# A recommendation tower on one Trainium2 core: its gram products split by weight columns into fourths of the TensorE array

## The chip, the core and the metric

The kernel runs on one NeuronCore of one Trainium2 chip. The metric is the device time of one launch in microseconds (us). TensorE (PE, its weight loads PEld) multiplies, VectorE (DVE) and ScalarE (ACT) work elementwise, GpSimd (POOL) and SyncE (SP) here issue transfers.

## The reference

There are 2048 samples. For each, 39 rows of 32 features are looked up in 39 tables. Everything is float32.

```python
def _cin_layer(h0, h, W):                      # Wr = W.reshape(F0, Fi, K)
    return jnp.einsum('bid,bjd,ijk->bkd', h0, h, Wr)
conv1 = _cin_layer(x, x, W1)                   # x: (2048, 39, 32), W1: (39*39, 128)
hidden1, final1 = conv1[:, :64, :], conv1[:, 64:, :]
conv2 = _cin_layer(x, hidden1, W2)             # W2: (39*64, 128)
z = jnp.sum(jnp.concatenate([final1, conv2], axis=1), axis=2)
h = jnp.concatenate([z, dense_ctx], axis=1)    # 192 + 16
h = jnp.maximum(h @ W_top1 + b_top1, 0.0)      # 512
h = jnp.maximum(h @ W_top2 + b_top2, 0.0)      # 256
y = h @ W_top3
```

Since `z` is summed over the 32 features, `final1` and `conv2` need only two small products per sample, summed over features: hidden with x (64 by 39) and x with x (39 by 39). These are the gram products that the change touches. `hidden1` itself is needed with its features.

## The kernel before

The samples go in 16 tiles of 128, each tile in two chunks of 64 samples, so there are 32 chunks. Two tiles are a pair, and each engine has a `pair_body` with `k` from 0 to 3 for the chunk in the pair and `t` from 0 to 6 for its seven steps. All queues are in order, and the order within them is written out by hand.

What one chunk goes through:

- POOL looks up 33 of the 39 tables for a tile by indirect transfers (L392), into `emb`, two buffers. It starts a tile's look-ups when the tile two earlier has been turned by DVE (`xt_ready`) and stored (`spilled`).
- SP stores the tile to DRAM in another order, 8 transfers of small rows (L341, "spill"), waits until they have landed, and then loads shifted copies of x, 14 transfers of 312 KB for each chunk (L359), into `copies`. Each load waits until DVE has made its last use of that buffer, two chunks earlier (one chunk for the last copy). The next tile's spill stands behind these 28 loads in the same queue.
- DVE multiplies pairs of copies (L750, four instructions a step; L745 in the last two chunks) into a ring of four places, three steps ahead of the step that PE is at. DVE also turns x (L726) and the hidden rows (L772).
- PE's `hidden_step` (L416) multiplies two weights by two blocks side by side, one in each column half of the array, and accumulates in `hidden`.
- ACT sorts the finished hidden rows (L586, L592), DVE turns them into `turned`, and one chunk later PE forms the gram products in `gram_group` (L439), after the steps `t` = 2, 4 and 6, for 3, 3 and 2 of eight parts. That is 6, 6 and 4 "places"; a place is one pair of matmuls, in the upper and the lower 64 rows of the array. ACT's `gram_copy` (L627) takes each group out of PSUM into `arena`; there is one PSUM place for all groups, so that the next group waits for it (`gram_out`).
- ACT's `spread_x` (L615) writes the diagonal operand `xdiag` for the coming gram products, part 0 at `t` = 4 and part 1 at `t` = 6.
- In odd chunks PE's `final_sums` (L456, then L461) follows each of the three gram groups. In even chunks `layer1` (L471, L472) follows the second and `layer2` (L480) the third; `layer3` (L487) stands in the odd chunk after the first group. The relus are ACT's `relu1` (L648) and `relu2` (L654). The first `final_sums` of an odd chunk also waits for `relu2` (`l2_act`), because both use the same PSUM bank.

Each float32 matmul shows in the trace as two PE records and two weight loads. A gram matmul before has 64 rows, 103 weight columns (64 of the summed hidden rows and 39 of x) and 78 streamed columns.

Of the kernel before, what the change touches and what calls it, by code (L numbers as in the profile page):

```python
# [16 lines left out]
HID = 64  # L17
# [16 lines left out]
LAST = STEPS - 1  # L34
# [9 lines left out]
GS = HID + F  # L44
GM = 2 * F
# [49 lines left out]
def since(count, first):  # L95
    return count >= first


def build(nc, dense, ids, hot_ids, hot_rows, tables, W_top1, b_top1, W_top2, b_top2, W_top3, W1, W2,
          fold_c, to_columns_c, to_samples_c, xt, hot_t, y_out):  # L100
    with ExitStack() as ctx:
        def sb(name, shape, dt):
            return ctx.enter_context(nc.sbuf_tensor(name, shape, dt))
# [7 lines left out]
        gst = [turned[:, u] for u in range(2)]  # L111
# [3 lines left out]
        xdiag = sb("xdiag", [P, HALF, GM], F32)  # L115
# [292 lines left out]
        def _(pe):  # L408
# [12 lines left out]
            def gram_group(k, chunk, j):  # L421
                if j == 0:
                    pe.wait_ge(hid_turned, 2 * chunk + 2)
                if j in (0, 2):
                    pe.wait_ge(xdiag_ready, 2 * chunk + 1 + j // 2)
                group = N_GROUPS * chunk + j
                into = gram
                if chunk == CHUNKS - 1 and j < 2:
                    into = hidden[:, j]
                elif chunk == CHUNKS - 1:  # L430
                    pe.wait_ge(gram_out, N_GROUPS * chunk)
                    pe.wait_ge(gram2_out, 1)
                elif since(group, 1):
                    pe.wait_ge(gram_out, group)
                for r in range(2 * GROUPS[j]):
                    place = 2 * sum(GROUPS[:j]) + r
                    for half in range(2):
                        rows = slice(64 * half, 64 * half + 64)
                        mm = nc.tensor.matmul(into[0:GS, half, r * GM:(r + 1) * GM],  # L439
                                              gst[k // 2][rows, 2 * place + k % 2, 0:GS],  # L440
                                              xdiag[rows, place, :], start=True, stop=True)
                mm.then_inc(gram_filled, 1)

            def final_sums(tile, u, j):
# [80 lines left out]
            for t in range(TILES):  # L525
                mm = nc.tensor.matmul(hidden[0:DENSE, t // 8, t // 4 % 2, (t % 4) * P:(t % 4 + 1) * P],
                                      dense_in[:, t, :], to_columns[:, :], start=True, stop=True)
# [34 lines left out]
            for p in range(1, PAIRS):  # L562
                pair_body(p, False)
            gram_group(3, CHUNKS - 1, 0)
            gram_group(3, CHUNKS - 1, 1)
            layer1(TILES - 2)
            gram_group(3, CHUNKS - 1, 2)
# [10 lines left out]
        def _(act):  # L578
            def sort_hidden(k, chunk):
                if since(chunk, 1):  # L580
                    act.wait_ge(hid_turned, 2 * chunk - 1)
                for bank in range(BANKS):
                    act.wait_ge(hid_pairs, pairs_done(chunk, LAST, bank))
                    for c in range(2):
                        q, other = 2 * c + bank, 2 * c + 1 - bank
                        op = nc.scalar.activation(hid_high[32 * q:32 * q + 32, :],  # L586
                                                  hidden[32 * other:32 * other + 32, k % 2, bank, :], ACT.Copy)
                op.then_inc(hid_sorted, 1)
                act.wait_ge(hid_sorted, 2 * chunk + 1)
                for q in (1, 3):  # L590
                    rows = slice(32 * q, 32 * q + 32)
                    op = nc.scalar.activation(hidden[rows, k % 2, 0, :], hidden[rows, k % 2, 1, :], ACT.Copy)  # L592
                op.then_inc(hid_sorted, 1)
# [10 lines left out]
            def spread_x(k, tile, chunk, part):  # L604
                places = slice(0, SPREAD) if part == 0 else slice(SPREAD, HALF)
                if part == 0 and k % 2 == 0:
                    act.wait_ge(xt_ready, tile + 1)
                    if tile + 2 < TILES:
                        act.wait_ge(spilled[tile % 2], 16 * SPILLS * (tile // 2 + 1))
                        place(tile + 2)  # L610
                if since(chunk, 1):
                    act.wait_ge(gram_filled, N_GROUPS * (chunk - 1) + 2 + part)
                for q in range(Q):
                    rows = slice(32 * q, 32 * q + 32)
                    op = nc.scalar.activation(  # L615
                        xdiag[rows, places, q % 2 * F:(q % 2 + 1) * F],
                        gst[k // 2][rows, 2 * places.start + k % 2:2 * places.stop:2, HID:GS], ACT.Copy)
                op.then_inc(xdiag_ready, 1)

            def gram_copy(k, tile, chunk, j):  # L620
                act.wait_ge(gram_filled, N_GROUPS * chunk + j + 1)
                if k % 2 == 0 and j == 0 and since(tile, 2):
                    act.wait_ge(fin_done, tile - 1)
                cols, g = gram_places(k, chunk, j)

                def copy(out, i, rows, last_copy=False):
                    op = nc.scalar.activation(out[:, :, cols].rearrange("p h (u b) -> p h u b", u=2), g[rows, i], ACT.Copy)  # L627
                    if last_copy:
                        op.then_inc(gram_out, 1)

                if not late(chunk, j):
                    copy(gram2[0:HID, :], slice(0, F, 2), slice(0, HID))
                    copy(gram2[HID:P, 0:FH - 1], slice(1, F, 2), slice(0, HID))
                for c in range(4):
                    rows = slice(c * SLOT, (c + 1) * SLOT)
                    copy(gram1[rows, 0:len(range(c, F, 4))], slice(c, F, 4), slice(HID, HID + SLOT))
                    rows = slice(c * SLOT, c * SLOT + TOP)
                    copy(gram1[rows, F1A:F1A + len(range(c, TOP, 4))], slice(SLOT + c, F, 4),
                         slice(HID + SLOT, GS), last_copy=(c == 3))

            def fin_half_copy(tile):
                act.wait_ge(fin_done, tile + 1)
                nc.scalar.activation(fin_half[:, :], fin_final1[64:128, :], ACT.Copy).then_inc(fin_half_out, 1)

            def relu1(tile):
                act.wait_ge(l1_done, tile + 1)
                for m in range(T1 // P):
                    op = nc.scalar.activation(act1[:, m, :], outs1[:, m, :], ACT.Relu, bias=bias1[:, m:m + 1])  # L648
                op.then_inc(l1_act, 1)

            def relu2(tile):
                act.wait_ge(l2_done, tile + 1)
                for m in range(T2 // P):
                    op = nc.scalar.activation(act2[:, m, :], outs2[:, m, :], ACT.Relu, bias=bias2[:, m:m + 1])  # L654
                op.then_inc(l2_act, 1)

            def pair_body(p, first):
                for k in range(4):
                    chunk, tile, done = 4 * p + k, 2 * p + k // 2, 2 * p - 2 + k // 2
                    for t in range(STEPS):  # L660
                        if t == LAST:
                            sort_hidden(k, chunk)
                            if chunk == CHUNKS - 1:
                                fin_half_copy(TILES - 2)
                        if t in (2, 4, 6) and (k or not first):
                            gram_copy((k - 1) % 4, 2 * p + (k - 1) // 2, chunk - 1, t // 2 - 1)
                        if k % 2 == 0 and not first and t == 4:
                            relu1(done)
                        if k == 1 and not first and t == LAST:
                            fin_half_copy(2 * p - 1)  # L670
                        if k == 3 and p < PAIRS - 1 and t == LAST:
                            fin_half_copy(2 * p)
                        if t in (4, 6):
                            spread_x(k, tile, chunk, t // 2 - 2)
                        if k % 2 == 0 and not first and t == LAST:
                            relu2(done)

            act.dma_start(row_number[:, :], hot_rows).then_inc(hot_loaded, 16)
            for n, f in enumerate(HOT):
# [21 lines left out]
            place(1)  # L701
            act.wait_ge(cleared, 3)
            pair_body(0, True)
            act.wait_ge(mlp_loaded, 16 * 7)
            for p in range(1, PAIRS):
                pair_body(p, False)
# [231 lines left out]
```

## Time and profile before

| | |
|---|---|
| time, median of 3 runs | 867.06 us (863.35 to 873.03) |
| the profiled execution's own time | 862.46 us |
| its span, first to last instruction | 860.7 us |
| mean granted TensorE clock | 0.966 |
| PE busy, of the span | 766.1 us (89%) |
| DVE busy | 702.1 us (82%) |
| ACT busy | 569.4 us (66%) |
| POOL busy | 536.1 us (62%) |
| gram products L439 (into `sums`): PE, weight loads | 115.1 us, 101.3 us |

An engine's busy time counts each moment once, however many of its records run in it. PE records are pipelined and start before the one ahead has ended, so that the spacing of their starts says more of a group's pace than the length of a record.

### The profile page before, as it was taken

The page shows a single profiled execution, that of the slowest core. Times are in us where ns is not written, and L with a number is a line of the kernel's source. Part 1 is how long each engine was busy: PE and PEld are TensorE (multiplying, and loading weights), DVE is VectorE, ACT ScalarE, POOL GpSimd, SP SyncE. Part 2 cuts the span into 40 slices and gives each one's busy share as a digit, 9 for nine tenths or more (in the row PEclk, how much of TensorE's full clock was granted, in tenths as well). Part 3 has the DMA queues.
Part 4 walks back from the last instruction along what each step waited for, and adds up shares of the span by engine and source line. Part 5 has one row for each costly group of instructions (what it writes and reads, how often), then busy time and mean ns, then how long its engine had stood idle before and what let it go on. Part 6 is the DMA issues. An engine that isn't in the chain of part 4 may idle for free.

```text
span 860.7 us, 17408 instructions
## 1 busy us (share of the span) xinstructions
PE 766.1 (89%) x6518; PEld 457.8 (53%) x6518; DVE 702.1 (82%) x1105; ACT 569.4 (66%) x1565; POOL 536.1 (62%) x535
## 2 busy tenths in 40 slices
PE   2696776899999998999899999999998989999996
PEld 1695122465556463645455564656464535556566
DVE  4957786899798979888889989898979787889850
ACT  0202244878777876767787878787876758787872
POOL 7777777777776777677676777777777676000000
PEclk9889896999999999999999999999999989999999
DMA  5759888788888888787878887888888788878300
GB/s 116 208 132 246 218 195 249 180 284 197 240 229 227 242 192 247 184 255 167 289 204 258 199 292 201 281 207 241 218 204 231 176 244 189 256 199 267 125 1 1
DMA packets 173739, 178.38 MB, mean 207 GB/s; under 512 B 144299, under 2 KB 154489, under 8 KB 156055
## 3 DMA queue, kind: packets, MB, share of 16 engines
q1 hardware_dynamic: 153243, 164.76, 67.6%
q0 software_dynamic: 16992, 8.73, 6.8%
q10 hardware_dynamic: 3420, 3.79, 1.5%
q8 instruction: 51, 0.84, 0.4%
q14 instruction: 33, 0.27, 0.1%
HBM read 161.97 MB, written 15.24 MB: 206 GB/s over the span
## 4 chain that ended last, share of the span: by engine, by line
PE 23%; ACT 22%; DMA 19%; DVE 17%; SPq 14%; issue 5%; DVEq 0%; ACTq 0%
DMA copies<-xt 14%; DVE blocks L750 13%; PE hidden L416 10%; ACT arena L627 9%; SPq L341 7%; PE sums L456 6%; SPq L359 6%; ACT xdiag L615 5%; PE sums L439 4%; ACT hid_high L586 4%; DMA blocks<-hot_t 3%; ACT hidden L592 2%; ACT act L648 2%; DMA xt<-emb 1%; DVE copies L805 1%
## 5 line engine op out<-in xcount | busy, mean ns | idle before, releaser
L392 POOL DMA_INDIRECT emb<-in_tbl,ids_tile x531 | 535.9, 1009 | 192.9 <-issue 188.8
L750 DVE TENSOR_TENSOR blocks<-copies 117x512 f32<-117x512 f32 x840 | 525.0, 693 | 96.4 <-PE hidden L416 45.1
L416 PE MATMUL hidden<-blocks,w_pairs 117*64 117x512 f32 x1792 | 439.3, 617 | 42.3 <-DVE blocks L750 40.0
L627 ACT ACTIVATE arena<-sums 64x480 f32<-64x480 f32 (+2 forms) x936 | 292.8, 313 | 178.4 <-PE sums L439 154.1
L416 PEld LDWEIGHTS hidden<-blocks,w_pairs 117*64 117x64 f32 x1792 | 145.0, 139 | 258.4 <-DVE blocks L750 112.8
L439 PEld LDWEIGHTS sums<-xdiag,turned 64*103 64x103 f32 x2000 | 101.3, 171 | 86.7 <-issue 39.4
L615 ACT ACTIVATE xdiag<-turned 32x468 f32<-32x468 f32 (+1 forms) x256 | 119.0, 465 | 3.4
L439 PE MATMUL sums<-xdiag,turned 64*103 64x78 f32 x2000 | 115.1, 261 | 6.8 <-ACT arena L627 5.7
L456 PE MATMUL sums<-arena,w_fin 128*128 128x128 f32 x640 | 81.7, 285 | 10.3 <-ACT act L654 9.7
L586 ACT ACTIVATE hid_high<-hidden 32x512 f32<-32x512 f32 x128 | 75.2, 588 | 16.3 <-PE hidden L416 14.3
L456 PEld LDWEIGHTS sums<-arena,w_fin 128*128 128x128 f32 x640 | 76.2, 197 | 13.4 <-issue 11.4
L726 DVE STREAM_TRANSPOSE turned<-emb 128x1248 f32<-128x1248 f32 x16 | 39.4, 2462 | 0.0
L592 ACT ACTIVATE hidden<-hidden 32x512 f32<-32x512 f32 x64 | 36.2, 566 | 1.4
L745 DVE TENSOR_TENSOR blocks<-copies 117x1024 f32<-117x1024 f32 x28 | 32.4, 1218 | 5.2 <-PE hidden L416 5.1
L480 PE MATMUL sums<-act,wt 128*128 128x128 f32 x256 | 32.8, 282 | 1.6 <-ACT act L648 1.2
L480 PEld LDWEIGHTS sums<-act,wt 128*128 128x128 f32 x256 | 29.8, 192 | 3.0 <-ACT act L648 1.4
L461 PE MATMUL sums<-arena,w_fin 128*64 128x128 f32 x384 | 30.9, 279 | 0.0
L471 PE MATMUL sums<-z_conv,wt1a 128*128 128x128 f32 x128 | 26.4, 287 | 1.1 <-DVE z_rest L781 1.1
L805 DVE TENSOR_SCALAR copies<-blocks,row_number 125x2048 bf16<-125x2048 int16 (+1 forms) x32 | 21.5, 742 | 5.1 <-DMA blocks<-hot_t 5.1
L461 PEld LDWEIGHTS sums<-arena,w_fin 128*64 128x64 f32 x384 | 23.4, 136 | 3.1
L472 PE MATMUL sums<-z_rest,wt1b 80*128 80x128 f32 x128 | 24.8, 274 | 0.0
L515 PE MATMUL sums<-turned,copies 125*128 125x96 bf16 x240 | 14.5, 236 | 9.4 <-DVE copies L805 4.7
(72 smaller groups left out, 294.9 us busy)
## 6 DMA issues: line engine op xcount, KB each, us to landing
copies<-xt SPq DMA_DIRECT2D x448, 312.0 KB
xt<-emb SPq DMA_DIRECT2D x64, 152.0 KB
emb<-in_tbl,ids_tile POOLq DMA_INDIRECT x531
xt<-emb SPq DMA_DIRECT2D x32, 104.0 KB
arena<-in_fold ACTq DMA_DIRECT2D x1, 2688.0 KB, 15.0
xt<-emb SPq DMA_DIRECT2D x32, 56.0 KB
blocks<-hot_t SPq DMA_DIRECT2D x3, 500.0 KB
turned<-hot_t SPq DMA_DIRECT2D x2, 468.8 KB
```

The source lines that it names most:

```text
L341: sp.dma_start(xt[u, row:row + end - first, h, :].rearrange("f (s d) -> s f d", d=D), emb[u][h::2, first * D:end * D].rearrange("s (f d) - ...
L392: pool.indirect_dma_start(out=emb[u][:, f * D:(f + 1) * D], out_offset=None, in_=tables[f], in_offset=bass.IndirectOffsetOnAxis(ap=ids_til ...
L416: mm = nc.tensor.matmul(hidden[64 * c:64 * c + 64, k % 2, bank, :], w_pairs[0:ROWS, t, bank * HALF_HID:bank * HALF_HID + HID], blocks[0:RO ...
L439: mm = nc.tensor.matmul(into[0:GS, half, r * GM:(r + 1) * GM], gst[k // 2][rows, 2 * place + k % 2, 0:GS], xdiag[rows, place, :], start=Tr ...
L456: mm = nc.tensor.matmul(fin_conv2, w_fin2[:, n, :], gram2[:, n, cols], start=(n == 0), stop=(n == FH - 1))
L461: mm = nc.tensor.matmul(fin_final1[64 * c:64 * c + 64, :], w_fin1[:, h, :], gram1[:, h, cols], start=(h < 2), stop=(h >= F1 - 2))
L480: mm = nc.tensor.matmul(outs2[:, m, :], wt2[:, c, m * P:(m + 1) * P], act1[:, c, :], start=(c == 0), stop=(c == T1 // P - 1))
L586: op = nc.scalar.activation(hid_high[32 * q:32 * q + 32, :], hidden[32 * other:32 * other + 32, k % 2, bank, :], ACT.Copy)
L592: op = nc.scalar.activation(hidden[rows, k % 2, 0, :], hidden[rows, k % 2, 1, :], ACT.Copy)
L615: op = nc.scalar.activation(xdiag[rows, places, q % 2 * F:(q % 2 + 1) * F], gst[k // 2][rows, 2 * places.start + k % 2:2 * places.stop:2, ...
L627: op = nc.scalar.activation(out[:, :, cols].rearrange("p h (u b) -> p h u b", u=2), g[rows, i], ACT.Copy)
L750: op = nc.vector.tensor_tensor(blocks[0:ROWS, at + c, :], a[:, cols], b[:, cols], ALU.mult)
```

## The change

Each gram matmul is cut into two by its weights' columns: 64 columns into PSUM partitions 0 to 63, and 39 columns into partitions 64 to 102. With the two halves of rows that makes four matmuls for a place, each in its own fourth of the array (64 rows by 64 columns). All four stream 78 columns as before. The outputs, their places and the semaphores stay; there are 2048 gram matmuls in place of 1024. On ACT, `relu2` moves ahead of part 1 of `spread_x` in the last step of even chunks.

```diff
@@ gram_group
                 for r in range(2 * GROUPS[j]):
                     place = 2 * sum(GROUPS[:j]) + r
-                    for half in range(2):
-                        rows = slice(64 * half, 64 * half + 64)
-                        mm = nc.tensor.matmul(into[0:GS, half, r * GM:(r + 1) * GM],
-                                              gst[k // 2][rows, 2 * place + k % 2, 0:GS],
-                                              xdiag[rows, place, :], start=True, stop=True)
+                    for features in (slice(0, HID), slice(HID, GS)):
+                        for half in range(2):
+                            rows = slice(64 * half, 64 * half + 64)
+                            mm = nc.tensor.matmul(into[features, half, r * GM:(r + 1) * GM],
+                                                  gst[k // 2][rows, 2 * place + k % 2, features],
+                                                  xdiag[rows, place, :], start=True, stop=True)
                 mm.then_inc(gram_filled, 1)
@@ ScalarE's pair_body
                             fin_half_copy(2 * p - 1)
                         if k == 3 and p < PAIRS - 1 and t == LAST:
                             fin_half_copy(2 * p)
+                        if k % 2 == 0 and not first and t == LAST:
+                            relu2(done)
                         if t in (4, 6):
                             spread_x(k, tile, chunk, t // 2 - 2)
-                        if k % 2 == 0 and not first and t == LAST:
-                            relu2(done)
```

## Rows read from the trace of the kernel before

**Rows 1.** Windows: whole middle, a calm tile, two others; busy us, clock, DMA share, GB/s.

```profile
178.20:780.30 602.10, 569.90 (x4422) 330.02 (x4421) 524.97 (x846) 460.60 (x1271) 401.50 (x398) 0.99 0.83 227
546.60:590.80 44.20, 42.91 (x342) 25.93 (x341) 40.41 (x66) 35.45 (x99) 33.34 (x34) 1.00 0.84 239
362.60:410.00 47.40, 44.48 (x343) 25.49 (x342) 40.45 (x68) 35.53 (x99) 33.38 (x33) 0.96 0.80 216
635.00:683.40 48.40, 44.29 (x342) 24.32 (x342) 40.38 (x67) 35.43 (x99) 35.63 (x35) 1.00 0.81 205
```

**Rows 2.** Waits of DVE, 125 to 780 us: total, times, longest.

```profile
DVE blocks L750 <- PE hidden L416: 45.1, 33, 3.8
DVE blocks L750 <- DMA copies<-xt: 39.4, 26, 3.5
```

**Rows 3.** Waits of SP's queue, 125 to 780 us.

```profile
SPq L359 <- DVE blocks L750: 28.2, 41, 3.7
SPq L359 <- DMA xt<-emb: 19.8, 13, 3.3
```

**Rows 4.** Timeline of SP's queue, 356.5 to 407 us: start, length, what.

```profile
356.57 22.34 SPq L359 DMA_DIRECT2D copies<-xt  x28
379.71 21.39 SPq L341 DMA_DIRECT2D xt<-emb  x8
401.15 0.63 SPq L364 DMA_DIRECT2D ids_tile<-in_ids  x1
405.13 2.41 SPq L359 DMA_DIRECT2D copies<-xt  x3
```

**Rows 5.** Timeline of SP's queue in a calm tile, from 558 us.

```profile
560.91 15.88 SPq L341 DMA_DIRECT2D xt<-emb  x8
576.83 0.63 SPq L364 DMA_DIRECT2D ids_tile<-in_ids  x1
578.68 25.66 SPq L359 DMA_DIRECT2D copies<-xt  x28
604.72 13.39 SPq L341 DMA_DIRECT2D xt<-emb  x2
```

**Rows 6.** Windows by phase of the transfers (last two columns: DMA share, GB/s).

```profile
358.00:395.00 37.00, 35.06 (x272) 19.84 (x270) 31.75 (x52) 26.51 (x71) 25.48 (x26) 0.95 0.86 254
395.00:404.00 9.00, 8.02 (x68) 5.11 (x66) 8.28 (x14) 8.68 (x27) 6.87 (x8) 1.00 0.76 122
404.00:406.00 2.00, 2.00 (x10) 0.62 (x10) 1.02 (x2) 0.27 (x2) 1.70 (x2) 1.00 0.15 19
538.00:571.00 33.00, 32.69 (x260) 20.13 (x258) 30.48 (x51) 24.61 (x73) 24.58 (x26) 1.00 0.88 284
```

**Rows 7.** Timeline of PE from 406 us: start, length of the group, what.

```profile
407.44 1.32 PE L439 MATMUL sums<-xdiag,turned 64*103 64x78 f32 x24
408.69 2.50 PE L456 MATMUL sums<-arena,w_fin 128*128 128x128 f32 x20
411.11 0.32 PE L461 MATMUL sums<-arena,w_fin 128*64 128x128 f32 x1
411.13 0.64 PE L416 MATMUL hidden<-blocks,w_pairs 117*64 117x512 f32 x1
...
414.91 0.95 PE L439 MATMUL sums<-xdiag,turned 64*103 64x78 f32 x16
415.79 1.42 PE L461 MATMUL sums<-arena,w_fin 128*64 128x128 f32 x21
```

**Rows 8.** Groups by form: busy us, mean ns of one record.

```profile
L439 PE MATMUL sums<-xdiag,turned 64*103 64x78 f32 x2000 | 115.1, 261 | 6.8 <-ACT arena L627 5.7
...
L487 PE MATMUL sums<-wt,act 128*128 128x1 f32 x64 | 8.3, 234 | 1.4 <-ACT act L654 0.7 <-DVE act L763 0.7
...
L520 PE MATMUL sums<-turned,copies 125*128 125x32 bf16 x48 | 1.5, 177 | 0.0
```

**Rows 9.** Timeline of PE in the calm tile, after the moved relu.

```profile
579.88 1.32 PE L439 MATMUL sums<-xdiag,turned 64*103 64x78 f32 x24 [0.26 <-ACT arena L627]
581.92 2.47 PE L456 MATMUL sums<-arena,w_fin 128*128 128x128 f32 x20 [0.72 <-ACT act L654]
```

**Rows 10.** Timeline of ACT in the same stretch.

```profile
576.88 2.87 ACT L627 ACTIVATE arena<-sums 64x320 f32<-64x320 f32 x10
579.77 1.37 ACT L615 ACTIVATE xdiag<-turned 32x156 f32<-32x156 f32 x4
581.16 0.62 ACT L654 ACTIVATE act<-sums,bias 128x128 f32<-128x128 f32 x2
```

**Rows 11.** Timeline of DVE in the same stretch.

```profile
575.46 2.50 DVE L750 TENSOR_TENSOR blocks<-copies 117x512 f32<-117x512 f32 x4 [1.29 <-PE hidden L416]
...
585.79 0.69 DVE L750 TENSOR_TENSOR blocks<-copies 117x512 f32<-117x512 f32 x1 [1.70 <-PE hidden L416]
```

## The prediction

> **What bounds the kernel now.** I read the busy shares tile by tile first. In the middle 602 us, 13 tiles, a tile takes 46.3 us. PE is busy 43.8 of them and DVE 40.4, and the transfers' share is 0.83. Tiles come in two kinds [rows 1]. Six of the 13 are calm, at 44.2 to 45.1 us, with PE idle 1.3 us in the one shown. The others take 47 to 48 us with the same PE work; there PE is idle 2.9 to 4.1 us. So PE paces the calm tiles, and something else adds about 3 us to the others.
>
> The waits name it. DVE waits 45.1 us for PE and 39.4 us for copies [rows 2]. SP's queue, which loads the copies, waits for DVE only 28.2 us in 655 [rows 3]. In a slow tile SP issues 28 loads in 22.34 us without a pause worth naming, then sits 21.39 us in eight spills, waits for them to land, and starts again: 405.13 less 356.57 is 48.6 us [rows 4]. Its spills are slow because the loads' data is still being moved. The loads fill 37 us at 254 GB/s and a share of 0.86, the spills' small rows 9 us at 122 GB/s, and then comes a lull of 2 us [rows 6]. In the calm tile the 28 loads did wait for DVE, 25.66 us in place of 22.34. Yet its spills took 15.88 in place of 21.39, and that cycle, spill to spill, is 43.8 us [rows 5]; the transfers ran at 0.88 and 284 GB/s meanwhile [rows 6]. What SP lost in waiting it got back in the spills. The reader is to see a loop of transfers that runs at its own pace, 43.8 to 48.6 us a tile, and PE beside it at about 44. The slower of the two sets each tile.
>
> **The change part by part.** *The gram products' pace.* 24 records start within 1.32 less 0.25 (one record's length), 1.07 us, and 16 within 0.70 [rows 7]. That is 45 ns a record, 181 ns for a place of four records. Two rows say what sets it. In L456, with 128 weight columns and 128 streamed columns, a record takes (2.50 - 0.28) / 20 = 111 ns [rows 7]. In L487, with 128 weight columns and one streamed column, it is still 8.3 us / 64 = 130 ns, tails included [rows 8]. So a load of 128 columns needs about 111 ns by itself, and one of 103 needs 111 x 103/128 = 89. The upper and lower rows load side by side, and 89 for two records is the 45 seen. The stream isn't the limit: L461 streams 128 columns in two column halves side by side at (1.42 - 0.27) / 21 = 55 ns a record, 110 a pair, with loads of 64 columns under it [rows 7]. So 78 columns want 67 ns.
>
> After the change loads have 64 or 39 columns (56 and 34 ns), the stream 67 ns. If all four fourths run together, a place takes two passes of 67, 134 ns in place of 181. No row shows four at a time. Rows side by side are shown by L439 itself, columns side by side by L461. Bounds for a place: 134 ns, and 2 x 134 = 268 if only two go at once. As the two kinds of neighbour are each shown, I take 134. It saves 47 ns x 16 places x 2 chunks = 1.5 us of PE a tile.
>
> *The number of records* doubles, 8 a place, so one must come every 17 ns. The shortest in the trace are L520's, 1.5 us / 48 = 31 ns each [rows 8], under weights of 128 columns, which the gram no longer has. Taken as a floor it would make a place 250 ns; I take no such floor, since two records in different column halves start 20 ns apart, at 411.11 and 411.13 [rows 7], though no row shows that kept up. The Trainium skill, TensorEngine Tiling (Array Packing), Instruction Overhead, gives each matmul about 60 cycles, whatever its free dimension. By that a place would take about 200 ns, an estimate from that page, and the change would cost PE 0.6 us a tile where I say it saves 1.5.
>
> *relu2 sooner.* The first final sums of an odd chunk start 0.72 us late, for relu2 [rows 9]. relu2 (0.62 us) ran after part 1 of the spreading (1.37 us) [rows 10]. Put first, it ends at about 580.4, before the gram group that precedes those sums, which starts at 579.88 and lasts over a microsecond. The wait goes, 0.7 us a tile. What moves back is the spreading, by 0.62 us; its reader is the third gram group of the next chunk, six steps later in PE's queue. ACT's total is the same, and the copies of the next group start when they did. Layer 2 stands three hidden steps ahead of the group at 579.88 in PE's queue, so relu2 finds it done.
>
> *What PE's 2.2 us are worth in a calm tile.* Not all reach DVE. The group at 579.88 waited 0.26 us for ACT's copies, a chain on ACT that the earlier four-place group doesn't shorten [rows 9, 10]. DVE's stalls on PE in that stretch are 1.29 and 1.70 us [rows 11]. I take 0.4 us off the first, 0.8 off the second and 0.4 in the odd chunk: 1.6 of 2.2, a PE-paced tile of 42.6 us.
>
> *What is late next: the transfers.* At 42.6 us PE is faster than the loop of transfers in every tile, 43.8 us at best. In the slow tiles nothing is gained, as a shorter stall on PE becomes a longer one on copies. In calm tiles 0.4 us is left. A tile's loads can come sooner by no more than SP's 28.2 us of waits in all, and the transfers' share was the same where it waited and where it didn't [rows 1, 3]. I take 3 us between 0 and 12, the latter if the six calm tiles keep their 1.6 us and the others 0.3.
>
> *The end.* After the last loads no transfer stands in the way. From about 745 us on, nearly two tiles, 2 x 1.6 = 3.2 us; the last stretch is ACT's copies, so I take 3. The 4096 added instructions cost fetches; nothing in the trace shows PE waiting for them: 0.
>
> Sum against the profiled execution: span 860.7, own time 862.46. 862.5 - 3 - 3 = 856.5 us. That execution lies 4.6 us under the median of 867.06. Against the median it is 861, rounded down to 860 since more of the unknown is gain than loss.
>
> **The rivals.** *The gain passes through.* If the loop of transfers follows DVE more than I think, the 1.6 us count in most tiles: 13 x 1.1 + 3 = 17 us, some 850. For it: DVE's 45.1 us on PE, and SP's waits. Against it: the slow tiles, where DVE waits for copies while SP doesn't pause.
>
> *Slower: only two fourths at a time.* A place takes 268 ns. PE gets 87 ns x 32 = 2.8 us more a tile, less 0.7 from relu2. A calm tile becomes 46.3 us; in the slow ones PE's idle time takes half of it. 6 x 2.1 + 7 x 1 + 4 at the end is 24 us: 891, or 884 if the slow tiles hide all of theirs. It decides from 181 + 0.7/32 us, 203 ns a place, on. The Trainium skill, TensorE: Matmul & The Clock Gate, Part 3, says that weight loads overlap running matmuls only when the row group differs. By that the column halves, which share their rows, couldn't overlap, and this rival would hold. L461 speaks against it: at 55 ns a record its loads must lie under matmuls of the same rows [rows 7].
>
> *The split does nothing.* Four records of halves take as long as two of wholes (160 to 200 ns a place). relu2's 0.7 us are left, mostly lost to the transfers, and 2 at the end: 863 to 866.
>
> **How the numbers follow.** Forecast (absorbed by transfers) 0.50, 855 to 865. Passes through 0.22, 845 to 855. Nothing 0.14. Slower 0.14, 872 to 895. The three runs shown spread by 1.1%, so 1% is about what can be told from no change. The range for 8 in 10 leaves out the far end of the slower rival and of the gain: 846 to 878. The forecast's own range is 855 to 865. Faster by over 1% means under 858.4: all of the second case and a quarter of the first, 0.34. Slower by over 1%: 0.14. The rest is 0.52.
>
> **What would show it.** The gram groups in PE's timeline: 48 records in some 1.05 us in place of 24 in 1.32, and 32 in 0.8. The idle time before L456 for L654 should vanish. DVE's waits for PE should fall by 15 to 25 us and those for copies rise by nearly as much; the middle tiles should not go under 43.5 us. A group of over 1.5 us would make the prediction wrong upward. Middle tiles at 42.6 us with DVE's waits for copies unchanged would make it wrong downward.

## The result, and the profile after

The changed kernel takes 869.96 us (median of 20 runs, 860.97 to 880.83), the kernel before 863.73 (20 runs, 852.61 to 873.36). The ratio is 1.0107 (95% interval 1.0071 to 1.0143): it is slower by about 1%, where I forecast 860 and some gain. The ratios here and below compare only the runs within 1.5% of each kernel's fastest, the medians take all of them. The profiled execution has a span of 863.2 us and a time of 864.95, one of the shorter ones.

PE's timeline over half a tile of the kernel after (start, length of the group, what, and in brackets the idle time before it):

```profile
252.94 1.03 PE L440 MATMUL sums<-xdiag,turned 64*64 64x78 f32 x48 [0.52 <-ACT arena L628]
253.90 2.50 PE L457 MATMUL sums<-arena,w_fin 128*128 128x128 f32 x20
256.24 0.51 PE L488 MATMUL sums<-wt,act 128*128 128x1 f32 x4
256.67 3.65 PE L416 MATMUL hidden<-blocks,w_pairs 117*64 117x512 f32 x16
260.26 1.06 PE L440 MATMUL sums<-xdiag,turned 64*64 64x78 f32 x48
...
267.48 0.76 PE L440 MATMUL sums<-xdiag,turned 64*64 64x78 f32 x32
```

48 records take 1.03 us where 24 took 1.32 [rows 7], and L457 follows without a wait where it stood 0.72 us for relu2 [rows 9]. ACT's timeline shows why: relu2 (L655) now stands ahead of the spreading (L616).

```profile
252.82 0.63 ACT L655 ACTIVATE act<-sums,bias 128x128 f32<-128x128 f32 x2
253.34 1.35 ACT L616 ACTIVATE xdiag<-turned 32x156 f32<-32x156 f32 x4
```

The groups (busy us, mean ns of one, idle time before and its cause) add it up: L440 is busy 90.9 us where L439 was 115.1 [rows 8], and the final sums have lost their wait.

```profile
L416 PE MATMUL hidden<-blocks,w_pairs 117*64 117x512 f32 x1792 | 451.1, 626 | 65.9 <-DVE blocks L751 61.7 <-issue 0.3
L440 PE MATMUL sums<-xdiag,turned 64*64 64x78 f32 (+1 forms) x4000 | 90.9, 235 | 8.8 <-ACT arena L628 7.2
L457 PE MATMUL sums<-arena,w_fin 128*128 128x128 f32 x640 | 81.1, 283 | 1.1 <-ACT arena L628 1.1
```

Where did PE's 24 us and relu2's 9 go? L416 took back 12 of them, 451.1 us for the same 1792 records, in place of 439.3 (most of it the clock, below). The rest is in DVE's and SP's waits from 125 to 780 us (total, times, longest):

```profile
DVE blocks L751 <- DMA copies<-xt: 65.7, 38, 5.2
DVE blocks L751 <- PE hidden L416: 25.3, 27, 2.4
...
SPq L359 <- DMA xt<-emb: 27.6, 14, 3.6
SPq L359 <- DVE blocks L751: 21.5, 47, 0.8
```

DVE waits for PE 19.8 us less than in [rows 2], and for copies 26.3 more. SP waits for DVE only 21.5 us, with no wait over 0.8, where there were 28.2 and one of 3.7 [rows 3]: DVE now hardly ever holds the loop of transfers. The windows (busy us of PE, PEld, DVE, ACT and POOL, then clock, DMA share, GB/s) say the same of the middle and of one tile of each kind:

```profile
178.20:780.30 602.10, 551.86 (x5932) 293.97 (x5930) 514.65 (x832) 453.17 (x1252) 402.21 (x399) 0.97 0.82 223
451.10:495.40 44.30, 42.11 (x470) 23.37 (x470) 40.43 (x66) 35.30 (x98) 31.85 (x33) 1.00 0.83 235
543.80:592.60 48.80, 44.02 (x470) 22.88 (x469) 40.31 (x67) 35.52 (x99) 33.06 (x33) 0.97 0.84 225
```

PE has fallen from 569.90 to 551.86 us of the 602.10 and DVE from 524.97 to 514.65 [rows 1]. What DVE does in a fixed stretch is progress, and it is 2% less. One transposition of the looked-up rows a tile marks the tiles in DVE's timeline. In the kernel after, two of them twelve tiles apart:

```profile
170.26 2.46 DVE L727 STREAM_TRANSPOSE turned<-emb 128x1248 f32<-128x1248 f32 x1
...
737.12 2.46 DVE L727 STREAM_TRANSPOSE turned<-emb 128x1248 f32<-128x1248 f32 x1
```

That is 566.86 / 12 = 47.2 us a tile. In the kernel before the same two stand at 178.20 and 734.96, 46.4 us a tile. These twelve tiles are 10.1 us longer after, and the next one 2.4, yet the two spans differ by 2.5 us: 7.9 us were saved ahead of the twelve and 2.1 behind the last tile's transposition. So a stretch of one profile isn't the kernel's loss.

### The profile page after: what moved, and what is told of

Its sections match the earlier page's. It is cut to its first block, busy times and chain, and to the rows that moved or that the text cites. A ratio compares the mean times of both kernels' runs of the same rounds, so it can differ in the third digit from the quotient of the medians.

```text
span 863.2 us, 21504 instructions
## 1 busy us (share of the span) xinstructions
PE 753.0 (87%) x8566; PEld 421.6 (49%) x8566; DVE 701.4 (81%) x1105; ACT 570.9 (66%) x1565; POOL 537.5 (62%) x535
## 4 chain that ended last, share of the span: by engine, by line
PE 21%; DMA 20%; ACT 19%; DVE 16%; SPq 9%; issue 4%; DVEq 0%; ACTq 0%
DMA copies<-xt 20%; DVE blocks L751 14%; ACT arena L628 9%; PE hidden L416 9%; SPq L359 7%; PE sums L457 5%; PE sums L440 4%; ACT hid_high L587 3%; ACT xdiag L616 3%; SPq L341 2%; ACT hidden L593 2%; ACT act L649 1%; DVE turned L773 1%; DVE blocks L746 1%; PE sums L481 1%
## 5 line engine op out<-in xcount | busy, mean ns | idle before, releaser
L416 PE MATMUL hidden<-blocks,w_pairs 117*64 117x512 f32 x1792 | 451.1, 626 | 65.9 <-DVE blocks L751 61.7
L416 PEld LDWEIGHTS hidden<-blocks,w_pairs 117*64 117x64 f32 x1792 | 134.8, 139 | 303.8 <-DVE blocks L751 177.0
L616 ACT ACTIVATE xdiag<-turned 32x468 f32<-32x468 f32 (+1 forms) x256 | 118.9, 464 | 3.1
L440 PEld LDWEIGHTS sums<-xdiag,turned 64*64 64x64 f32 (+1 forms) x4000 | 76.2, 125 | 90.4 <-issue 48.9
L440 PE MATMUL sums<-xdiag,turned 64*64 64x78 f32 (+1 forms) x4000 | 90.9, 235 | 8.8 <-ACT arena L628 7.2
L457 PE MATMUL sums<-arena,w_fin 128*128 128x128 f32 x640 | 81.1, 283 | 1.1 <-ACT arena L628 1.1
L457 PEld LDWEIGHTS sums<-arena,w_fin 128*128 128x128 f32 x640 | 75.2, 195 | 3.9 <-ACT arena L628 1.2
L462 PE MATMUL sums<-arena,w_fin 128*64 128x128 f32 x384 | 30.9, 279 | 0.0
L462 PEld LDWEIGHTS sums<-arena,w_fin 128*64 128x64 f32 x384 | 23.4, 136 | 3.2
```

The costliest lines, as they stand in the source:

```text
L416: mm = nc.tensor.matmul(hidden[64 * c:64 * c + 64, k % 2, bank, :], w_pairs[0:ROWS, t, bank * HALF_HID:bank * HALF_HID + HID], blocks[0:RO ...
L440: mm = nc.tensor.matmul(into[features, half, r * GM:(r + 1) * GM], gst[k // 2][rows, 2 * place + k % 2, features], xdiag[rows, place, :], ...
L457: mm = nc.tensor.matmul(fin_conv2, w_fin2[:, n, :], gram2[:, n, cols], start=(n == 0), stop=(n == FH - 1))
L462: mm = nc.tensor.matmul(fin_final1[64 * c:64 * c + 64, :], w_fin1[:, h, :], gram1[:, h, cols], start=(h < 2), stop=(h >= F1 - 2))
L616: op = nc.scalar.activation(xdiag[rows, places, q % 2 * F:(q % 2 + 1) * F], gst[k // 2][rows, 2 * places.start + k % 2:2 * places.stop:2, ...
```

## The experiments

**First and second set: the parts, each by itself.** Theories: (A) the loop of transfers holds the end and PE's pace is nothing, either way; (B) the added records cost the transfers something, through their fetches; (C) PE's new pace or the new order costs it; (D) the two parts do it only together.

`e1` moves relu2 alone, `e2` splits alone. `e3` and `e4` separate pace from number of records, both with relu2 moved:

```
e3: for features in (slice(0, HID), slice(HID, GS)):   # split as in the change
      cols = GM if r == 2 * GROUPS[j] - 1 else 104     # stream 104 columns, not 78
      matmul(into[features, half, r*GM : r*GM + cols], ..., flat xdiag[place*GM : +cols])
e4: for half in range(2):                              # not split: 2 records a product
      matmul(into[0:HID, half, ...], gst[...][rows, ..., 0:HID], xdiag[rows, place, :])
```

In e3 the columns beyond 78 fall on the next place, which is written afterwards. e4 leaves out the 39 weight columns of x, so x by x isn't computed. Its loads are short, and it has the change's pace with the old number of records.

> Only relu2 is moved ahead of the spreading; the gram products are as before. Three theories of why the changed kernel is 1.07% slower although its gram products run at 136 ns a place in place of 181. Fetch theory: the 4096 added PE instructions are fetched by more transfers of 16 KB, which fall among the spills' small rows and lengthen the loop of transfers; then this kernel, with no instruction added, is 0.997 to 1.000 of before. Pace theory: a faster PE makes DVE follow the copies closely, SP's queue no longer waits for DVE, and the loop of transfers runs less well by itself; then this one, which gives PE a third of the change's gain, is 1.002 to 1.005. Order theory: the later spreading costs the time; then this one is 1.010.

> Only the gram products are split; relu2 stays where it was. Fetch theory: as slow as the full change less the relu's gain, 1.010 to 1.015. Pace theory: 1.005 to 1.010. Order theory: 1.000 or under.

> The full change, but each split gram matmul streams 104 columns in place of 78 (except the last place of a group; the surplus columns are overwritten by the next place), so that a place takes about 178 ns, as before the change, with the doubled instructions. Fetch theory: still slow, 1.010 to 1.020. Pace theory: PE has its old pace but for relu2, so 1.000 to 1.003, with SP's waits for DVE back near 28 us.

> Gram products unsplit, but with the 64 weight columns of the hidden rows alone (the products of x with x are left out), relu2 moved as in the change. A place should take about 136 ns, the pace of the changed kernel, with the instruction count of the kernel before. Fetch theory: 0.990 to 1.000 of before. Pace theory: as slow as the change, 1.007 to 1.014.

> The full change once more, on the same chip and against the same runs of before as the next three. If the 1.07% of the first comparison is the change's, 1.005 to 1.015 again. If it was the chip's drift, about 1.000.

> The unsplit fast gram (64 weight columns only, the products of x with x left out, relu2 moved), the changed kernel's pace with the old count of instructions, now beside the full change. Fetch theory: 0.4 to 1% under the full change's time. Pace theory: the same time as the full change.

| kernel | gram pace | records | median us, before on its chip | ratio (95%) |
|---|---|---|---|---|
| e1 relu2 alone | old | single | 865.91, 867.39 | 1.0022 (0.9967 to 1.0076) |
| e2 split alone | new | double | 868.47, 867.39 | 1.0001 (0.9924 to 1.0078) |
| e3 slow split | old | double | 872.35, 867.39 | 1.0135 (1.0073 to 1.0196) |
| e4 fast whole | new | single | 868.61, 867.39 | 1.0000 (0.9925 to 1.0074) |
| e5 the change again | new | double | 867.18, 863.87 | 1.0039 (0.9989 to 1.0089) |
| e6 fast whole again | new | single | 861.93, 863.87 | 0.9962 (0.9902 to 1.0023) |

e3's group is busy 110.6 us, near the 115.1 of before. Group L439 of e4 shows that it has the new pace, and 24 of its records take 1.03 us:

```profile
L439 PE MATMUL sums<-xdiag,turned 64*64 64x78 f32 x2000 | 93.1, 239 | 8.2 <-ACT arena L627 7.0
```

And its row of the queue that fetches instructions (packets, MB, share) that it has the old number of fetches, the kernel after's row standing under it:

```profile
q8 instruction: 51, 0.84, 0.4%
```

```profile
q8 instruction: 67, 1.10, 0.5%
```

e4's waits moved just as the change's did (DVE for copies, for PE):

```profile
DVE blocks L750 <- DMA copies<-xt: 61.5, 36, 3.3
DVE blocks L750 <- PE hidden L416: 28.6, 32, 2.5
```

Read it as a table of two by two, all four with relu2 moved. The two measurements of the change, weighted by their intervals, give 1.0084 ± 0.0029; those of e4 and e6 give 0.9977 ± 0.0047. Doubling the records costs the mean of (1.0135 - 1.0022) and (1.0084 - 0.9977), 1.1% ± 0.5, some 9 us. The new pace gives the mean of (1.0084 - 1.0135) and (0.9977 - 1.0022), -0.5% ± 0.5, some 4 us. The medians of the table give less: 0.7% for the records (6 us), and nothing for the pace (0.05% slower). e3 makes the largest part of the difference, 1.0135 by its ratio and 1.0057 by its median, from six runs. The sign of the records' cost holds by either count, its size and the gain by pace don't. (A) falls: the added records aren't indifferent. (C)'s pace falls: faster products cost nothing. (B) is supported in that records cost time; that it is by their fetches isn't shown by this. Against it stands e2, which doubles the records and shows no loss. Its interval ends at 1.0078, under the 1.010 to 1.015 that was set down for it. A loss of 0.6%, records less pace, still fits in. (D) can't be shut out. e2 does show relu2's wait left in place: `14.1 <-ACT act L655` stands before its L457.

**Where the time goes in the loop of transfers.** In the tail of each cycle, from the last copy's data to the next tile's first load, only spills and gathers move, in rows under 512 bytes. The rows of the DMA queues (packets, MB, share) of such a tail in the kernel after, 392.3 to 400.3 us:

```profile
q1 hardware_dynamic: 5692, 0.72, 58.4%
q0 software_dynamic: 218, 0.11, 9.2%
q8 instruction: 1, 0.02, 0.8%
```

It took 8.0 us and held a fetch of instructions, one packet of 16 KB. That from 579.8 to 586.2 took 6.4 and held none:

```profile
q1 hardware_dynamic: 5760, 0.73, 74.8%
q0 software_dynamic: 170, 0.08, 8.2%
```

I read 12 tails in each of ten profiles (before, after, e1 to e8), from the issue times of SP and the times of the packets. The 51 without such a packet took 6.60 us in the mean, the 69 with one or more 7.61. In the kernel before a cycle was 46.44 us, of it 6.85 in the tail with 0.42 fetches each; in the one after 47.47, 7.53 and 0.83. Over all ten, kernels with single records have 0.49 a tail and those with doubled ones 0.71. 0.22 times 1.0 us is 0.2 us a tile, 3 us in all: a third of the 9.

The whole cycles, though, don't follow the records. With single records they took 46.44 (before), 46.69 (e1), 46.55 (e6) and 47.43 us (e4), with doubled ones 47.47 (after), 46.67 (e2), 47.35 (e3) and 47.09 (e5). e4, which has the old number of fetches and a ratio of 1.0000, has as long a cycle as the change.

**Third: is it the size of the packet?** `e7` puts one packet of 11.5 KB into each tail of the kernel before, `e8` one of 64 bytes.

```
e7, e8: between the first and the second part of the spill, from tile 2 on:
+ sp.dma_start(extra[tile:tile + 1, 0:2880], row[:, 0:2880])      # e8: 0:16
```

> The kernel before, with one more transfer for each tile from the third on: one row of 11.5 KB from SBUF to a scratch place in DRAM, issued between the first and the second part of the spills (from results nobody reads; nothing is left out). It stands in for an instruction fetch of 16 KB in the spills' phase. If one large packet among the small rows holds their landing up, the phase from the last copy to the next first load grows by 0.6 to 1 us a tile beyond the control (the next kernel), and the time by 8 to 14 us, 1.01 to 1.016 of before. If not, as the control.

> The control: the same added transfer with 64 bytes. It costs its issue in SP's queue, some 0.6 us in a loop of 46 us a tile, so 1.000 to 1.010, and at least 0.5% less than with 11.5 KB if the packet's size matters.

e7 took 870.85 us, ratio 1.0063 (1.0004 to 1.0121), and e8 870.20 (six runs, from 851.96 to 873.75) beside 863.87. By their medians the two are alike, 6 to 7 us over before: the size of the added packet made no difference that can be told, and the large one did not stand in for a fetch. e8 has no interval, and its runs spread over 22 us. Whether it is the fetch's packet that delays a tail, or whether both fall late for another reason, isn't shown.

**Fourth: a steeper dose of records, and half the loads.** `e9` splits into eight parts of 32 columns and less (16 records a place). `e11` and `e12` are the kernels before and after with half of each copy's columns loaded:

```
e9: for features in (slice(0, 32), slice(32, HID), slice(HID, 96), slice(96, GS)):
e11, e12: sp.dma_start(x_copy[...][g::THIRDS, 0:COLS // 2], xt[u, r:r + F, k, 0:COLS // 2])
```

In these the other half of each copy keeps what stood there. On the chip that ran this set the kernel before took 1452.05 us, on that of the next 1469.84; what they show is told as theirs.

> The full change taken one step further: each gram product in four column parts (32, 32, 32 and 7 columns), eight matmuls for a place, each in an eighth of the array, so that PE's instructions grow by 8192 more where the change added 4096. Fetch theory: dose and effect go together; if the change costs 0.4 to 0.8%, this one costs 1.2 to 2.4%, with 0.9 or more 16 KB fetches in the spills' phase of a tile. If a place also gets slower than 181 ns (16 records in it, 8 ns apart are needed for 134 ns), that is seen in the gram groups and told apart by DVE's waits for PE. Order theory: as the full change, 1.007.

> The split with relu2 in its old place, once more. Fetch theory: 1.004 to 1.010, as the full change. Order theory (the later spreading costs 0.8% when the gram is split): 1.000 as at the first time.

> The kernel before with each copy's load cut to half of its columns (the other half of the products is from old data), so that the transfers are no bound. PE then paces every tile at the calm tiles' 44.2 us: 13 x (46.3 - 44.2) = 27 us less, some 835 us, 0.965 of before. DVE's waits for copies near 0.

> The changed kernel with the same halved loads. If the change's gain on PE is real and only the transfers hide it, a tile takes 42.6 us and this one is 1.6 x 14 + 3 = 20 to 28 us under the halved kernel before, 0.935 to 0.945 of before. If the added instructions cost time on PE or its queue itself, it is no faster than the halved kernel before.

> The full change beside the split alone on one chip. Fetch theory: both 1.003 to 1.010, equal within 0.3%. Order theory (the moved relu2 hurts once the gram is split): 1.008, and 0.5% or more over the split alone.

> The split with relu2 in its old place. Fetch theory: as the full change. Order theory: 1.000.

> The kernel before with each copy's load cut to half of its columns (half of the products come from old data). The transfers are no bound: PE paces every tile at 44.2 us, some 835 us, 0.965 of before, DVE's waits for copies near 0. Had it been something else than transfers that adds 2 us to the mean tile, it would stay at 1.00.

> The full change with the same halved loads. If the gain on PE is real and only the transfers hide it: a tile of 42.6 us, 20 to 28 us under the halved kernel before, 0.935 to 0.945 of before. If the added instructions cost PE itself time: no faster than the halved kernel before.

| kernel | median us | ratio (95%) |
|---|---|---|
| e9 eighths | 1487.89 | 1.025 (1.0223 to 1.0278) |
| e10 split alone | 1453.2 | 1.0007 (0.9986 to 1.0028) |
| e11 before, half loads | 1458.09 | 1.0042 (1.0016 to 1.0068) |
| e12 after, half loads | 1445.56 | 0.9961 (0.9944 to 0.9978) |
| e13 the change (1469.84 before) | 1440.63 | 0.9808 (0.9775 to 0.9841) |
| e14 split alone (1469.84) | 1460.98 | 0.994 (0.992 to 0.9961) |
| e15 before, half loads (1469.84) | 1475.95 | 1.0039 (1.0014 to 1.0064) |
| e16 after, half loads (1469.84) | 1450.04 | 0.9866 (0.9821 to 0.9911) |

Here the volume of the loads is nothing (e11, e15). SP's timeline in e11 shows the spills issued by 576.4, and the next tile's first load only at 608.31:

```profile
559.95 3.82 SPq L359 DMA_DIRECT2D copies<-xt  x5
565.75 10.62 SPq L341 DMA_DIRECT2D xt<-emb  x8
577.07 0.71 SPq L364 DMA_DIRECT2D ids_tile<-in_ids  x1
608.31 2.38 SPq L359 DMA_DIRECT2D copies<-xt  x3
```

It isn't the spills' landing that SP waits for. Their last packet ended at 574.46, while SP's wait ended at 608.26, right behind an instruction of DVE (608.24) that used the buffer to be loaded. DVE had stood still before that, though the last packet of the loads had ended at 566.29:

```profile
599.59 2.65 DVE L750 TENSOR_TENSOR blocks<-copies 117x512 f32<-117x512 f32 x4 [41.81 <-remote]
603.38 4.86 DVE L750 TENSOR_TENSOR blocks<-copies 117x512 f32<-117x512 f32 x8
```

SP's waits over the run say the same, `SPq L353 <- DVE blocks L750: 365.2, 12, 32.6`. From 576.5 to 607 us the transfer engines moved 9 GB/s. PE did nothing from 576 to 599 us either, so the copies are what DVE waited for: on these chips it goes on some 30 us after their last packet (in e13 the same two stand at 570.77 and 601.49). The loop is then a serial one, copies, DVE, SP, copies, and PE's pace counts in DVE's part. e13 got 29.2 us out of it over 16 tiles, 1.8 a tile, near my 2.2. Its parts don't come out, however: the split alone (e14) got 8.9 us, 0.6 a tile where I had 1.5, and on the other chip (e10) nothing, so that relu2's move would have been worth 20 us, 1.3 a tile, where I had 0.7.

e9 is slower. A place of 16 records is no faster than one of 8: 96 records start within 1.23 - 0.22 = 1.01 us, 10.5 ns each, 168 ns a place where the fourths take 134.

```profile
294.52 1.23 PE L440 MATMUL sums<-xdiag,turned 64*32 64x78 f32 x96
```

And L440 waits 242 us for nothing but "issue", L462, which the edit doesn't touch, another 193; in e10, with half the records, these were 21.1 and 0.3. Most of that isn't lost, since PE's wait for DVE at L416 fell from 454.1 us in e10 to 14.0. Whether the longer places or these waits make e9 slower isn't shown. That chip's late copies are in it, so it says nothing of the dose on a usual one.

```profile
L440 PE MATMUL sums<-xdiag,turned 64*32 64x78 f32 (+1 forms) x8000 | 154.7, 234 | 250.6 <-issue 242.2 <-ACT arena L628 8.0
L462 PE MATMUL sums<-arena,w_fin 128*64 128x128 f32 x384 | 84.7, 369 | 193.3 <-issue 193.0
```

**Fifth: half the loads on a chip of the usual time** (864.47 before).

> The kernel before with each copy's load cut to half of its columns. On a chip at the usual speed: transfers are no bound, PE paces every tile at 44.2 us, some 835 us, 0.965 of before, DVE's waits for copies near 0. On the slow-landing chip: 1.004, as before.

> The full change with the same halved loads. At the usual speed: a tile of 42.6 us, 20 to 28 us under the halved kernel before, if the gain on PE is real and only transfers take it. POOL's look-ups, 33 times 1.25 us and their hand-over, need some 43 us a tile and may hold it at 43: then 15 us. If the added instructions cost PE itself time: no faster.

e17, before with half the loads, took 817.64 us (0.9401, 0.9284 to 0.9518) and e18, the change with half the loads, 793.89 (0.9155, 0.9062 to 0.9248): 23.7 us less for the change by the medians, 2.6% by the ratios, well outside both intervals. The window 178.2 to 700 us of e17:

```profile
178.20:700.00 521.80, 506.17 (x4026) 307.43 (x4026) 475.33 (x765) 419.19 (x1153) 396.17 (x399) 1.00 0.54 136
```

And of e18:

```profile
178.20:700.00 521.80, 507.34 (x5689) 296.78 (x5690) 490.73 (x792) 433.88 (x1196) 400.63 (x398) 1.00 0.56 140
```

PE is busy 97% in both, at full clock, and DVE gets 3.2% more done. DVE's waits (total, times, longest) hold none for copies; the first row is e17's:

```profile
DVE blocks L750 <- PE hidden L416: 51.1, 40, 3.1
```

```profile
DVE blocks L751 <- PE hidden L416: 33.0, 40, 1.4
```

The transpositions of the same two tiles, twelve apart, in e17:

```profile
160.03 2.46 DVE L726 STREAM_TRANSPOSE turned<-emb 128x1248 f32<-128x1248 f32 x1
...
691.03 2.47 DVE L726 STREAM_TRANSPOSE turned<-emb 128x1248 f32<-128x1248 f32 x1
```

and in e18:

```profile
157.61 2.46 DVE L727 STREAM_TRANSPOSE turned<-emb 128x1248 f32<-128x1248 f32 x1
...
671.90 2.47 DVE L727 STREAM_TRANSPOSE turned<-emb 128x1248 f32<-128x1248 f32 x1
```

44.25 us a tile before, 42.86 after: 1.4 us. With PE alone setting the tile, the change is worth what its parts promise. e18 has the doubled records too, so where the transfers have room they cost nothing that shows. With the full loads all of it is gone, and more.

## Why the prediction was wrong

**The pace of a place: right.** 134 ns were forecast. Between the starts of 48 records lie 1.03 - 0.23 = 0.80 us, 17 ns each, 67 for four, 134 for a place of eight. The rival of two fourths at a time (268 ns) is out. So is the rule of the Trainium skill that backed it (TensorE: Matmul & The Clock Gate, Part 3: loads overlap matmuls only where the row group differs): half of each four share their rows, and they do overlap.

**No floor of 31 ns: right.** 17 ns a record held over 48 of them. The 60 cycles a matmul of the Trainium skill (TensorEngine Tiling (Array Packing), Instruction Overhead) would make it 25 ns at 2.4 GHz and a group 1.2 us, an estimate from that page; the trace has 1.03.

**relu2: right.** The 0.72 us before L457 are gone (1.1 us left in all of 10.3), and nothing that was moved back came late.

**PE's 2.2 us worth 1.6 in a PE-paced tile: right mechanism, slightly too much.** e17 and e18 measured 1.4.

**The end: right.** From the last tile's transposition to the end of the span it is 860.7 - 780.31 = 80.4 us before and 863.2 - 784.90 = 78.3 after. I had 3 us for nearly two tiles.

**What failed: "the transfers ... I take 3 us", with "the 4096 added instructions cost fetches ... 0" behind it.** The first half held: DVE's waits for PE fell by 19.8 us (15 to 25 forecast) and came back as waits for copies. But I took the loop of transfers as a fixed thing, 43.8 us at best, that could only leave a gain of 0 to 12. It didn't leave one: the kernel lost 6.2 us by the medians. My test for the instructions was whether PE waits for them. It doesn't (`issue 0.3` at L416), but that looked at the wrong engine: the fetches are moved by the same transfer engines that bound the kernel. The two by two puts the added records at +1.1% ± 0.5 by the ratios and +0.7% by the medians, against a gain by pace of 0.5% ± 0.5 or nothing, where I summed 6 us. The term taken as 0 was some 6 to 9 us; by what way the records cost it stays open. One reading was off besides: I called PE's work the same in both kinds of tile, but it is 44.48 and 44.29 us busy in the slow ones and 42.91 in the calm one [rows 1], so waiting was only about half of their 3 us.

**What stays open.** By the tails, fetches account for about 3 of the 9 us, but an added packet of 11.5 KB cost no more than one of 64 bytes. A second candidate for the rest is the clock. Between 178 and 780 us the granted clock dipped to half, the level of 1.2 GHz, 9 times in the profile after and 3 times before. A record of L416 took 1065 ns in a dip and 592 (median) outside; 80 and 60 of them over the whole span fell in one, which makes 9 of L416's 12 us. But e4 has 8 such dips, an L416 of 451.7 us and no loss. Ahead of each of the 12 dips PE had just stood idle for 1.4 to 2.9 us, so they may as well follow from a longer loop as cause it. The third is that split and move hurt only together: e2 and e1, each alone, show none. The intervals leave room for it. No kernel with more doubled records and full loads was run on a usual chip, and the cycles of single profiles can't settle it, with e4 at 47.43 us and e2 at 46.67.

**Slower as a case.** I gave it 0.14 and one mechanism, on PE. No rival of mine let the transfers get slower, so the sign was missed though the range held the time.

## What to carry to other kernels

Where two engines set the tile by turns, price a change at what the other one allows, and then ask what the change adds to the other one's load: here 16 fetches more of 16 KB, on the transfer engines. To see whether a gain on one engine is real, lighten the other and measure the pair again: half the loads turned +1% into -2.6%. The count of instructions can be a cost of its own: the same pace with single records (e4 and e6, which leave some products out) came out at 0.9977 where the change has 1.0084, even though PE hardly waited for an instruction (0.3 us of `issue` at L416).

## What the runs showed of the hardware

- Four products in four fourths of the array (64 rows by 64 or 39 columns each, float32, 78 columns streamed) run at once: a record every 17 ns, over 48 records. With eight products (e9) a record came every 10.5 ns, which made a place longer, 168 ns in place of 134.
- Instruction fetches are visible transfers of 16 KB in one packet (16 more for 4096 more instructions, so 256 each). The Trainium skill (Runtime: NRT & Kernel Launch, Instruction fetch mechanics) gives that size and calls the fetch mostly hidden. For PE the usual chip agrees (0.3 us of `issue` at L416). A fetch took its engine 1.13 us in the profile before.
- PE can creep while it waits for nothing that the profile shows. In e9 it made 41 records at full pace from 301.90 us, then crept:

```profile
301.90 0.71 PE L440 MATMUL sums<-xdiag,turned 64*32 64x78 f32 x41
302.84 0.33 PE L440 MATMUL sums<-xdiag,turned 64*32 64x78 f32 x5 [0.24 <-issue]
...
330.89 0.29 PE L440 MATMUL sums<-xdiag,turned 64*32 64x78 f32 x1 [2.51 <-issue]
333.68 0.28 PE L440 MATMUL sums<-xdiag,turned 64*7 64x78 f32 x1 [2.51 <-issue]
...
348.39 1.98 PE L462 MATMUL sums<-arena,w_fin 128*64 128x128 f32 x16 [0.23 <-issue]
```

  In the window from 302 to 344 us no packet of q8 moved; from 344 to 350 one did, and PE was back at full pace. It fits a fetch that is seen late on that chip, as the copies are; that, and why it crept and did not stop, nothing here shows.
- Two chips ran the kernel before in 1452 and 1470 us in place of 864, with the copies used only about 30 us after their last packet. There the ratio of the same change was 0.9808, so a comparison holds for the kind of chip that it was made on.
